# Scatter-adding every expert unit into one result tensor instead of two alternating ones

## The reference

```
x = x + _L0_xattn_ref(_layernorm(x, axis=-1), ctx_2048, mask_BxS2_bk0)
x = x + _L0_ffn_ref(_layernorm(x, axis=-1), ...)
...
    order = jnp.argsort(flat_e)
    tok = order // TOP_K
    xs = x[tok]
    gu = lax.ragged_dot(xs, jnp.swapaxes(gate_up_proj, 1, 2), group_sizes)
    gate, up = jnp.split(gu, 2, axis=-1)
    hact = jax.nn.silu(gate) * up
    y = lax.ragged_dot(hact, jnp.swapaxes(down_proj, 1, 2), group_sizes)
    out = jnp.zeros_like(x).at[tok].add(y * w[:, None])
```

## Time and profile before

| | before |
|---|---|
| median of 3 runs | 839.45 us |
| lowest, highest | 837.8 us, 840.26 us |
| profiled execution: span from first to last instruction | 805.3 us |
| median less span (start and end of an execution, outside the trace) | 34.2 us |
| busy share of the span: PE, DVE, ACT, POOL | 84%, 67%, 56%, 64% |
| bytes moved by DMA | 189.93 MB |

### The profile page before, as it was taken

One profiled execution on the slowest core, in us unless ns is written; L12 is line 12 of the kernel. 1 busy time (PEld: TensorE's weight loads), 2 busy tenths in 40 slices (PEclk: granted clock), 3 DMA queues, 4 the chain that ended last, 5 costly groups with the idle time before them and its releaser, 6 DMA issues. The chain is left out here.

```text
span 805.3 us, 15215 instructions
## 1 busy us (share of the span) xinstructions
PE 676.6 (84%) x4278; PEld 560.5 (70%) x4278; DVE 541.6 (67%) x1213; ACT 450.7 (56%) x891; POOL 516.2 (64%) x461
## 2 busy tenths in 40 slices
PE   4999999630599999999998998999988998989730
PEld 2555565320589999888988888878877977878630
DVE  5699898861276667776677777776767777767611
ACT  3444454310366666666775766757666676666610
POOL 6037777776738877887766666676657666666421
PEclk9999999855599999999999999999999999999965
DMA  8999999505659999999999999999999999999576
GB/s 304 349 313 332 322 330 301 170 12 159 177 154 220 244 240 237 239 247 255 247 268 256 268 241 259 245 245 258 236 260 217 250 236 245 233 246 232 107 132 152
DMA packets 107557, 189.93 MB, mean 236 GB/s; under 512 B 33521, under 2 KB 35441, under 8 KB 106065
## 3 DMA queue, kind: packets, MB, share of 16 engines
q1 hardware_dynamic: 74274, 125.61, 50.2%
q0 software_dynamic: 33200, 63.35, 38.9%
HBM read 143.40 MB, written 56.24 MB: 248 GB/s over the span
## 5 line engine op out<-in xcount | busy, mean ns | idle before, releaser
L1223 PE MATMUL bank<-xh,w1h 128*128 128x256 f32 (+7 forms) x768 | 229.3, 299 | 21.4 <-DVE h L887 21.2
L1224 PE MATMUL bank<-xl,w1h 128*128 128x256 f32 (+7 forms) x768 | 220.5, 287 | 0.0
L1225 PE MATMUL bank<-xh,w1l 128*128 128x256 f32 (+7 forms) x768 | 220.4, 287 | 0.0
L608 POOL DMA_INDIRECT xg<-normed_tokens,list x145 | 159.3, 1099 | 62.5 <-issue 55.9
L1223 PEld LDWEIGHTS bank<-xh,w1h 128*128 128x128 f32 x768 | 147.5, 192 | 27.0 <-issue 26.7
L617 POOL DMA_INDIRECT out_rows<-ys,list x73 | 116.7, 1599 | 72.9 <-ACT ys L1040 60.4
L903 DVE TENSOR_TENSOR xl<-bank,xh 128x448 fp32r<-128x448 f32 (+3 forms) x145 | 84.3, 616 | 115.1 <-ACT xh L1047 115.0
L592 POOL DMA_INDIRECT list_table<-token,slot x112 | 112.4, 1004 | 69.7 <-ACT token L1001 35.9
L617 POOL DMA_INDIRECT second_sum<-ys,list x70 | 111.2, 1589 | 64.5 <-ACT ys L1040 43.5
L1224 PEld LDWEIGHTS bank<-xl,w1h 128*128 128x128 f32 x768 | 147.9, 193 | 0.1
L1225 PEld LDWEIGHTS bank<-xh,w1l 128*128 128x128 f32 x768 | 147.6, 192 | 0.0
(11 more groups left out here) (204 smaller groups left out, 1084.7 us busy)
## 6 DMA issues: line engine op xcount, KB each, us to landing
raw<-in_w SPq DMA_DIRECT2D x195, 256.0 KB, 4.7
raw<-in_w2a SPq DMA_DIRECT2D x65, 256.0 KB, 5.0
ctxT_s<-in_ctxT SPq DMA_DIRECT2D x16, 768.0 KB, 7.3
ctx_s<-in_ctx SPq DMA_DIRECT2D x16, 768.0 KB, 8.8
raw<-in_w2b SPq DMA_DIRECT2D x65, 128.0 KB, 5.9
list_table<-blank SPq DMA_DIRECT2D x30, 256.0 KB, 7.6
x_in<-in_x SPq DMA_DIRECT2D x16, 224.0 KB, 4.5
out_rows<-x SPq DMA_DIRECT2D x16, 224.0 KB, 8.8
```

The source lines that it names most:

```text
L608: pool.indirect_dma_start(xg[u.on(XGS)][0:u.m, t, :], None, normed, bass.IndirectOffsetOnAxis(ap=lists[u.on(LISTS)][0:u.m, t, 0:1], axis=0 ...
L1223: pe.matmul(bank[m][:, 0:W], wh, mh, start=(c == 0), stop=False)
L1224: pe.matmul(bank[m][:, 0:W], wh, ml, start=False, stop=False)
L1225: mm = pe.matmul(bank[m][:, 0:W], wl, mh, start=False, stop=(c == DK - 1))
```

## The change

All units add to `out`. `second_sum`, its zeroing, the buffer of zeros and the final 3.5 MB addition go. One semaphore `scattered` counts all landings, and the scatter of unit u waits until all units before it, unit u - 1 among them, have landed. The over units get a semaphore of their own (`over_added`), and `keep_list` waits for its list instead of for scatters.

```
-    def sums(self):
-        return self.slot % 2
-
     def landed(self, back):
 
-        upto = max(self.slot - back + 1, 0)
-        tiles = sum(nt for v, (nt, m) in enumerate(RANKED[:upto]) if v % 2 == (self.slot - back) % 2)
-        return tiles * 16
+        return TILES_BEFORE[max(self.slot - back + 1, 0)] * 16
 
     def landed_before(self):
 
-        tiles = sum(nt for v, (nt, m) in enumerate(RANKED[:self.slot]) if v % 2 == self.slot % 2)
-        return tiles * 16 if not self.loop else (self.n - self.slot + tiles) * 16
+        return self.t0 * 16
...
-            def clear_sum(i):
-                sp.dma_start(second[i * P:(i + 1) * P, :], zeros[:, 0:D]).then_inc(cleared_sum, 16)
-
...
-                    wait(sp, scattered[u.sums()], u.landed(LISTS))
+                    wait(sp, scattered, u.landed(LISTS))
...
-            nc.gpsimd.memset(zeros[:], 0.0).then_inc(const_pool, 1)
...
             def scatter(u):
 
-                split_wait(pool, scattered[u.sums()], u.landed_before())
+                wait(pool, scattered, u.landed_before())
                 for t in range(u.nt):
-                    split_wait(pool, ys_s, u.t0 + t + 1)
-                    pool.indirect_dma_start((out, second)[u.sums()], bass.IndirectOffsetOnAxis(ap=lists[u.on(LISTS)][0:u.m, t, 0:1], axis=0),
+                    pool.wait_ge(ys_s, u.t0 + t + 1)
+                    pool.indirect_dma_start(out, bass.IndirectOffsetOnAxis(ap=lists[u.on(LISTS)][0:u.m, t, 0:1], axis=0),
                                             ys[u.on(2)][0:u.m, t, :], None, compute_op=ALU.add, bounds_check=TOK - 1, oob_is_err=False
-                                            ).then_inc(scattered[u.sums()], 16)
+                                            ).then_inc(scattered, 16)
...
             def keep_list(u):
-                split_wait(pool, scattered[u.sums()], u.landed_before())
+                split_wait(pool, list_in[u.on(LISTS)], (u.turn(LISTS) + 1) * 16)
...
-                pool.wait_ge(merged, 16)
+                pool.wait_ge(scattered, TILES_BEFORE[STATIC] * 16)
                 pool.indirect_dma_start(out, bass.IndirectOffsetOnAxis(ap=over_list[:], axis=0),
                                         ys[u.on(2)][0:u.m, 0, :], None, compute_op=ALU.add, bounds_check=TOK - 1, oob_is_err=False
-                                        ).then_inc(scattered[u.sums()], 16)
-
-            for i in range(2):
-                pool.wait_ge(scattered[i], SUM_TILES[i] * 16)
-            pool.dma_start(out[0:TOK, :], second[0:TOK, :], accum_op=ALU.add, max_dma_last_dim=8192).then_inc(merged, 16)
+                                        ).then_inc(over_added, 16)
+                split_wait(pool, over_added, (u.n - STATIC + 1) * 16)
...
                 if u.loop:
                     split_wait(act, kept, (u.n - STATIC + 1) * KEPT)
-                wait(act, scattered[u.sums()], u.landed_before() if u.loop else u.landed(2))
+                    act.wait_ge(scattered, TILES_BEFORE[STATIC - 1] * 16)
+                else:
+                    wait(act, scattered, u.landed(2))
```

More of the change, by code:

```diff
@@ L67 @@
 TILES_BEFORE = [sum(nt for nt, m in RANKED[:u]) for u in range(STATIC + 1)]
-SUM_TILES = [sum(nt for nt, m in RANKED[i::2]) for i in range(2)]
 WIDE = max(nt * m for nt, m in RANKED)
@@ L147, in program @@
     table = nc.dram_tensor("list_table", (PAD_LIST + BLANKS, LINE), I32, kind="Internal").ap()
-    second = nc.dram_tensor("second_sum", (TOK, D), F32, kind="Internal").ap()
     normed = nc.dram_tensor("normed_tokens", (TOK, D), F32, kind="Internal").ap()
@@ L196, in program @@
         row = sb("row", [P, 1])
-        zeros = sb("zeros", [P, D])
         blank = sb("blank", [P, BLANKS, LINE], I32)
@@ L290, in program @@
         list_in = [sem(f"list_in{i}") for i in range(LISTS)]
-        gathered = [[sem(f"gathered{i}_{t}") for t in range(3)] for i in range(XGS)]; scattered = sem2("scattered"); cleared_sum = sem("cleared_sum"); merged = sem("merged"); kept = sem("kept")
+        gathered = [[sem(f"gathered{i}_{t}") for t in range(3)] for i in range(XGS)]; scattered = sem("scattered"); over_added = sem("over_added"); kept = sem("kept")
         w1h_s = sem("w1h_s"); w1l_s = sem("w1l_s"); w2h_s = sem("w2h_s"); w2l_s = sem("w2l_s")
@@ L404, in _ @@
         def _(sp):
-            CLEAR_AT = [B - 1, B, B + 1]
             def load_x(b):
@@ L433, in fill_lists @@
                     sp.dma_start(per_expert[e:e + quarter, i * BLANKS * LINE:(i + 1) * BLANKS * LINE], source).then_inc(done, 16)
-            def clear_sum(i):
-                sp.dma_start(second[i * P:(i + 1) * P, :], zeros[:, 0:D]).then_inc(cleared_sum, 16)
             def slot(s):
-                if s.n in CLEAR_AT:
-                    for i in range(CLEAR_AT.index(s.n) * TOK // P // len(CLEAR_AT), (CLEAR_AT.index(s.n) + 1) * TOK // P // len(CLEAR_AT)):
-                        clear_sum(i)
                 batches(s, (-4, load_x), (-2, load_ctxT), (-1, load_ctx))
@@ L446, in slot @@
                 if s.n == 0:
-                    sp.wait_ge(const_pool, 2 + PADS // BLANKS)
+                    sp.wait_ge(const_pool, 1 + PADS // BLANKS)
                     sp.dma_start(table[PAD_LIST:PAD_LIST + BLANKS].rearrange("(o n) c -> o (n c)", o=1),
@@ L515, in _ @@
             overs = over_loop(sp, lambda u: None, next_over)
-            sp.wait_ge(scattered[0], SUM_TILES[0] * 16)
-            split_wait(sp, scattered[1], (overs + SUM_TILES[1]) * 16)
-            sp.wait_ge(merged, 16)
+            sp.wait_ge(scattered, TILES_BEFORE[STATIC] * 16)
+            split_wait(sp, over_added, overs * 16)
             split_wait(sp, list_in[LAST.on(LISTS)], (overs + LAST.turn(LISTS) + 1) * 16)
@@ L541, in _ @@
                                channel_multiplier=0).then_inc(const_pool, 1)
-            pool.wait_ge(const_pool, 2 + PADS // BLANKS)
+            pool.wait_ge(const_pool, 1 + PADS // BLANKS)
             nc.gpsimd.memset(tri[:], -1.0).then_inc(cleared, 1)
@@ L600, in _ @@
                 pool.wait_ge(x1_out[i], stores * 16)
-            pool.wait_ge(cleared_sum, TOK // P * 16)
             pool.wait_ge(c_plan, PLAN_STATIC)
@@ L1262 @@
 DVE_CONSTS = 13 + len(CAP_STEPS)
-CONSTS = 19 + PADS // BLANKS + XGS + 3 * NSENT
+CONSTS = 18 + PADS // BLANKS + XGS + 3 * NSENT
 NOVERS = 2 * E + 2 * MAX_OVER
```

## The result

| | before | after |
|---|---|---|
| median of 4 runs | 838.62 us | 907.12 us |
| lowest, highest | 837.38, 840.26 us | 902.06, 913.11 us |
| ratio of after to before, 95% interval | | 1.0819 [1.077, 1.0868] |
| profiled execution: span | 805.3 us | 906.6 us |

The change costs 0.0819 x 838.62 = 68.7 us (64.6 to 72.8). Ratios leave out runs more than 1.5% above the fastest of the same kernel; medians and ranges are of all runs.

A forecast was written before the change was run, and what follows sets the result against it. PE and the DMA engines were taken as both near their limit in phase 2, PE setting the beat. +56 us for the new wait and -17 for the tail gave +39 on 839.45: 878 us, range 848 to 911 (8 in 10).

The forecast's parts named there:

- The forecast's own case: Whole kernel: 35 to 69 us added by the waiting scatters, 17 taken; 857 to 891 us, likeliest 878; chance 0.67.
- no relief at all: Rival: loaded turns stay long and POOL's longer release adds 12 us: 69 + 12 - 17 = +64, 903 us; chance 0.22.
- What bounds the kernel now: Phase 2: PE and DMA engines near their limit; PE sets the beat, 8.46 us for 2 x 128.
- The new wait, loaded bound of 69 us: Phase 2: scatters become a strict sequence; with landings unchanged, each turn's excess over PE's beat adds 69 us together.
- The relief of 13 us: Phase 2: beat grows about an eighth at equal bytes, shortening turns near 0.2 us a unit, some 13 us over 60 units.
- Who stands behind it: Phase 2: POOL's gathers wait behind the scatter and PE for them, some 40 us and more idle; ACT and SP as before.
- The tail, -17 us: After the last scatter: without the merge the over scatter starts 16.9 us earlier, what follows stays the same; 17 us saved.
- Phase 1, 0: Phase 1: the zeroing runs beside POOL's list-table DMAs and costs nothing, uncovered less than 1 us; taken as 0.
- The base: Whole kernel: the 34.2 us between the profiled span of 805.3 and the median lie outside the trace, unchanged.
- The quick landing: Rival, phase 2: landings come near their quiet 4.4 us, nothing is added, 822 us; chance 0.07.
- the page's fixed cost: Skill page's price for a GpSimd DMA: about 2.0 us plus bytes at 436 GB/s; turn 5.5 us, only the 17 us show.
- my own quiet bound of 7.3 us: Two-tile turn in a quiet queue: 1.94 issue + 4.4 landing + 0.94 POOL release, below each two-tile beat, excess 0.

The follow-up runs named there:

- the wait alone: Kernel before with each scatter waiting for the landings of all earlier units; both sums, zeroing and final addition kept: 917.88 us, ratio 1.0916.
- The run with 16 places: Changed kernel with a list ring of 16 places instead of 8, bytes the same: 868.84 us, ratio 1.0284 to the kernel before.
- the addition alone: Kernel before without the final addition of the second sum, so rows are missing in the output: 825.34 us, ratio 0.984.
- the second profile: Kernel before, unedited, profiled once more: the execution took 835.72 us with a span of 833.9 us.
- small weights: Changed kernel fetching only 16 numbers per partition of each weight load after the first units: 823.26 us, ratio 0.9807 to the kernel before.

## Why the prediction was right, and where its sizes were not

The direction, the mechanism and the range were right: 878 was predicted, 848 to 911, and 907.12 measured. The forecast's own case ended at 891; the rival nearest to the result is "no relief at all" with 903. That it came so near is in part luck: it put 12 us more on a release of POOL that is 0.2 us longer than SP's, and the two start 0.06 us apart, some 4 us over 60 units, while its 69 us were too small.

*What bounds the kernel now*: right. Both PE and the DMA engines were full, and a landing was hidden behind another unit's turn. Reading the turn from SP's list load was right as well: in after list load and scatter start 0.06 us apart.

*The new wait, loaded bound of 69 us*: right in kind and too small. The profiles show 85 us, and the wait alone cost 76.8. By classes, expected and measured: 3 x 112, 12.0 and 10.9; 3 x 96, 12.0 and 13.4; 2 x 128, 17.8 and 20.6; 2 x 112, 16.8 and 25.0; 2 x 96, 10.6 and 15.5. Two steps made it small. The 2 x 112 units got the excess of their neighbours, 1.05 us, and show 1.56. The beat of 2 x 96 was read from one pair, 7.93; the mean is 7.53, so that their excess is 1.29 instead of 1.06.

*The relief of 13 us, which made 56 of the 69*: this is the step that failed. "The beat grows by about an eighth while the bytes per unit stay" is true, and the DMA share did fall, to 0.79 to 0.85. (An eighth of 2.2 us is 0.28, not "near 0.2", so its own rule gives 16 us.) But a turn did not get shorter with it: 9.67 us in 2 x 128 against the 9.5 read in the full stage. The sentence ahead of it had given the likely reason, that one landing releases list, weights and the next scatter; the mean share then says nothing of what a scatter meets. The run with 16 places puts 45 us on this coincidence by the times, 29 by its profile, and leaves the 2 x 128 turn where it was. The burst was also larger than foreseen: the second weights, timed by PE before (L463 in before), now go out in it, some 4.0 us after a first scatter of 2 x 128 instead of 6.5.

*Who stands behind it*: right for POOL's gathers and PE, with 77.1 us idle before line 1186 in phase 2 where "some 40 us and more" were expected. Wrong for ACT, which now does wait for landings before `ys`, 30.9 us in 21 waits; that should cost nothing of its own, because the scatter behind it waits for a later landing anyway, but no run tests it. SP's list wait asks for the same unit as before, as said, but it is no longer idle time of no consequence: it sets when the weights go out.

*The tail, -17 us*: the mechanism is right, the size a bit large. The profiles give -16.2; the addition alone timed -13.4. The over scatter came 7.2 us after the last scatter, where "some 10" were expected; that is 19.4 us sooner than in the second profile, not 16.9. But what follows it was not "the same": it took 11.8 us instead of 8.5. The two errors nearly cancel, which is luck.

*Phase 1, 0*: the first scatter starts 2.7 us later than in the second profile of before. Among the other kernels it starts between 265.2 and 275.8 us, so this is not told from no change.

*The base*: wrong in its reason. The 34.2 us are not outside the trace; the profiled execution was quicker. Because the sum was made of differences inside one profile, nothing of it changed.

*The quick landing and the page's fixed cost*: these fall. The Trainium skill's page "DMA: Bandwidth & Descriptors", section "Anatomy of one DMA — SWDGE (gpsimd) path", prices a DMA by a constant and its bytes. It gave an estimate of 5.5 us for a turn of two tiles of 128 rows. The landings ended turns of 8.99 us in the rows of after and of 8.2 to 8.9 even with small weights, so the trace does not agree, and my own quiet bound of 7.3 us was not reached there either. That bound also counts POOL's release twice: 773.31 is the start of an instruction of POOL, so that the 4.4 us hold the release already, and the rows give 1.94 + 4.42 = 6.4. By the rule of the eighth the relief would then have been some 23 us, further still from what was measured.

## What to carry to other kernels

A buffer or tensor that looks like a spare copy may be what takes a long landing off the path: before merging two accumulators, read one turn "issue, land, release" in the loaded stage and compare it with the beat, class by class, for the excess is paid by every unit. When one event releases both a transfer on the path and a burst of other transfers, the mean DMA share is no guide to how fast that transfer will be; price it by a turn in the burst, and expect no relief because the loop got slower. A loop that then stays slow can be helped by giving the burst another release (here a longer list ring, worth 29 to 45 us), though here the second tensor with its 13 us addition is cheaper than any of it.

## What the runs showed of the hardware

- In the strict sequence with the weights beside it, an accumulating scatter gives 82 us of excess over 63 units and an overwriting one of the same rows some 4 us (times, with the tail's 13.4 us added).
- The DMA share of the 2 x 128 stage fell from 1.00 to 0.85, and the turn of the scatter that runs in it did not get shorter: 9.18 and 9.83 us in two units before, 9.67 in the mean after.
- Most of a turn is the last landing, with or without weights beside it: in after the second scatter of 559.19 lands at 565.44, 6.25 us later, and the next unit's starts 0.81 us behind that; with small weights five such landings take 5.5 to 6.1 us.
- PE's granted clock, 1.00 in the 2 x 128 and 2 x 112 stages before, has a mean of 0.95 and 0.88 in after: a part of each stage ran at the 1.2 GHz level, while PE was idle for 26 of 164 us and 24 of 156. With small weights the 2 x 128 stage is back at 1.00. The time lost by it was not measured; PE has idle time beside it.
- Phase 1 of the same kernel can differ by 29 us between two executions (first scatter at 236.6 and 265.8 us): a single profile's total is not a base for a sum.
